# The experts' SiLU in a Mamba block with experts: one ScalarE function in place of tanh and a VectorE operation

## What is computed

```python
g = jnp.einsum('th,eih->tei', x, gate_proj)
u = jnp.einsum('th,eih->tei', x, up_proj)
act = jax.nn.silu(g) * u
expert_out = jnp.einsum('tei,ehi->teh', act, down_proj)
y = jnp.einsum('teh,te->th', expert_out, combine)
# and in the mixer, for each token:
A_bar = jnp.exp(dt_t[:, :, None] * A)
h = A_bar * h + (dt_t * x_t)[:, :, None] * B_t[:, None, :]
y_t = jnp.einsum('bdn,bn->bd', h, C_t)
```

## Time and profile before

| what | us |
|---|---|
| median of 3 runs (2777.73 to 2789.72) | 2781.56 |
| span of the profiled execution | 2779.7 |
| VectorE busy | 2424.8 |
| TensorE busy | 2379.4 |
| GpSimd busy | 2234.5 |
| ScalarE busy | 1565.3 |

### The profile page before, as it was taken

The page is one execution under the profiler, slowest core; times in us unless marked ns, Lnnn a source line. Parts: engine busy times, 40 slices in busy tenths (PEclk is TensorE's granted clock), DMA queues, the critical chain, the costliest instruction groups (busy, mean ns, idle before and its releaser), DMA issues.

```text
span 2779.7 us, 29004 instructions
## 1 busy us (share of the span) xinstructions
PE 2379.4 (86%) x9004; PEld 1687.3 (61%) x9004; DVE 2424.8 (87%) x2450; ACT 1565.3 (56%) x2961; POOL 2234.5 (80%) x1563
## 2 busy tenths in 40 slices
PE   3445798998989899898989999898999989898899
PEld 1222466666756666675666667666666756666678
DVE  2688999999999999999999999999999999999922
ACT  3556666566566656655665655566565556665311
POOL 1578888888888888888898888888888888987922
PEclk8677899999999899999999999999999999999999
DMA  4689898999989899998989989898998989898921
GB/s 113 172 209 231 220 236 219 229 237 218 239 221 235 218 227 235 222 236 214 234 224 238 232 220 244 213 233 218 241 231 218 241 205 235 222 245 210 241 64 50
DMA packets 338380, 596.80 MB, mean 215 GB/s; under 512 B 49696, under 2 KB 160288, under 8 KB 338224
## 3 DMA queue, kind: packets, MB, share of 16 engines
q0 software_dynamic: 72960, 243.30, 45.6%
q1 hardware_dynamic: 265264, 351.64, 40.3%
HBM read 349.89 MB, written 10.06 MB: 129 GB/s over the span
## 4 chain that ended last, share of the span: by engine, by line
PE 25%; POOL 22%; issue 17%; DVE 17%; ACT 10%; DMA 8%; SPq 0%; POOLq 0%; DVEq 0%; ACTq 0%
POOL unit L1199 9%; PE wbank L498 7%; DVE hbank L726 7%; DMA gsum<-unit 4%; POOL act L1166 4%; POOL gsum L1211 3%; PE mbank L510 3%; PE wbank L440 3%; DVE unit L740 3%; PE wbank L526 2%; PE wbank L388 2%; ACT z L849 2%; PE wbank L460 2%; DMA w_all<-w_scratch 2%; ACT hbank L1028 2%
## 5 line engine op out<-in xcount | busy, mean ns | idle before, releaser
L1199 POOL TENSOR_TENSOR unit<-dtx,b_bc 128x1024 f32<-128x1024 f32 x512 | 1345.9, 2639 | 10.8 <-DMA b_bc<-bc_scratch 8.9
L726 DVE TENSOR_TENSOR_SCAN hbank<-hbank,unit 128x1024 f32<-128x1024 f32 x512 | 1173.2, 2291 | 72.7 <-ACT hbank L1028 66.4
L1028 ACT ACTIVATE hbank<-dt,a_neg 128x512 f32<-128x512 f32 x1024 | 668.8, 681 | 303.6 <-DVE unit L740 269.6
L510 PE MATMUL mbank<-down_t,act 128*128 128x256 f32 x2048 | 525.6, 394 | 69.5 <-POOL act L1166 46.7
L740 DVE TENSOR_TENSOR unit<-hbank,c_bc 128x1024 f32<-128x1024 f32 x448 | 546.2, 1219 | 25.9 <-DVE hbank L726 1.8
L1166 POOL TENSOR_TENSOR act<-act,w_all 128x512 f32<-128x512 f32 x256 | 359.6, 1405 | 242.6 <-DVE act L704 222.9
L1211 POOL DMA_DIRECT2D gsum<-unit x448 | 444.0, 991 | 105.0 <-DMA gsum<-unit 50.8
L498 PE MATMUL wbank<-h_t,up_t 128*128 128x256 f32 x2048 | 503.6, 390 | 10.7 <-DVE gz L608 10.7
L510 PEld LDWEIGHTS mbank<-down_t,act 128*128 128x128 f32 x2048 | 397.5, 197 | 176.2 <-issue 64.8
L498 PE MATMUL wbank<-h_t,gate_t 128*128 128x256 f32 x2048 | 489.4, 382 | 13.4 <-DVE dt L600 11.4
L498 PEld LDWEIGHTS wbank<-h_t,up_t 128*128 128x128 f32 x2048 | 396.0, 195 | 108.8 <-DVE gz L608 29.2
(11 more groups left out here) (121 smaller groups left out, 2398.2 us busy)
## 6 DMA issues: line engine op xcount, KB each, us to landing
gsum<-unit POOLq DMA_DIRECT2D x448, 512.0 KB, 7.3
c_bc<-bc_scratch SPq DMA_DIRECT2D x464, 256.0 KB, 5.6
b_bc<-bc_scratch SPq DMA_DIRECT2D x448, 256.0 KB, 6.2
w_all<-w_scratch SPq DMA_DIRECT2D x256, 256.0 KB, 4.6
ht<-in_L_attn_x_dram SPq DMA_DIRECT2D x16, 512.0 KB, 6.0
w_out<-in_L_attn_W_out_dram SPq DMA_DIRECT2D x16, 512.0 KB, 6.2
ht<-in_L_attn_x_dram POOLq DMA_DIRECT2D x16, 512.0 KB, 8.4
out_dram<-xt SPq DMA_DIRECT2D x16, 512.0 KB, 3.3
```

Of the source, the lines that this page charges most:

```text
L510: m = eng.matmul(mbank[:, u * H:(u + 1) * H], act[:, (n - 1) % MOE_RING, j, u * P:(u + 1) * P], down_t[:, e, :], start=(e == 0 and u == 0) ...
L726: eng.tensor_tensor_scan(h, h, unit[:, g % RING, :, :].rearrange("p a t -> p (a t)"), 0.0, ALU.mult, ALU.add).then_inc(scanned, 1)
L1028: eng.activation(hbank[g % HB][:, a, :], dt[:, 2 * q + a, :], ACT.Exp, scale=a_neg[:, 2 * q + a, n:n + 1]).then_inc(decayed, 1)
L1199: eng.tensor_tensor(unit[:, g % RING, :, :], dtx[:, 2 * q:2 * q + 2, :], b_bc[:, s:s + 1, :].to_broadcast([P, 2, T]), ALU.mult).then_inc(d ...
```

## The change

The experts' function on ScalarE is Silu in place of tanh of half the value. It writes straight into `act` and frees the gate bank; the tile `etanh`, its semaphore and VectorE's (tanh + 1) * gate are gone. VectorE's product with the up product waits for Silu through the semaphore of the gate bank. The down weights are no longer halved. ScalarE has to load a table where it goes from Silu to Exp, Tanh or Ln and back.

```diff
--- before.py
+++ after.py
@@ -164,7 +164,6 @@
         rows_out = sb("rows_out", [BC, T])
         mod_row = conv[:, 1, :].rearrange("p (a h) -> p a h", h=H)
         act = sb("act", [P, MOE_RING, 2, HT])
-        etanh = sb("etanh", [P, 2 * HT])
         w_all = sb("w_all", [P, W_RING, 2, HT])
 
         sums = sb("sums", [P, TT])
@@ -231,8 +230,8 @@
         rnorm_a, rnorm_p, rnormed = sem("rnorm_a"), sem("rnorm_p"), sem("rnormed")
         driven, decayed, scanned, c_scaled = (sem(n) for n in ("driven", "decayed", "scanned", "c_scaled"))
         summed = [sem(f"summed{k}") for k in range(2)]
-        etanhed, weighted, down_done, moe_v, moe_out = (
-            sem(n) for n in ("etanhed", "weighted", "down_done", "moe_v", "moe_out"))
+        weighted, down_done, moe_v, moe_out = (
+            sem(n) for n in ("weighted", "down_done", "moe_v", "moe_out"))
         work = Banks(wbank, [sem(f"work{k}_full") for k in range(3)], [sem(f"work{k}_free") for k in range(3)])
 
 
@@ -690,15 +689,9 @@
                 for s in range(E + 1):
                     n = E * row + s
                     a = act[:, n % MOE_RING, :, :].rearrange("p j t -> p (j t)")
+                    yield
                     if s < E:
-
-                        t = work.at["gates2", row, s]
-                        need.wait_ge(etanhed, n + 1)
-                        eng.scalar_tensor_tensor(out=a, in0=etanh[:, :], scalar=1.0, in1=t.bank[:, :], op0=ALU.add,
-                                                 op1=ALU.mult).then_inc(t.free, 1)
-                    yield
-                    if s < E:
-                        g, t = t, work.at["ups2", row, s]
+                        g, t = work.at["gates2", row, s], work.at["ups2", row, s]
                         need.wait_ge(t.full, t.after)
                         need.wait_ge(g.free, g.after)
                         eng.tensor_tensor(a, a, t.bank[:, :], ALU.mult).then_inc(t.free, 1)
@@ -755,7 +748,7 @@
                     o = dst[:, 2:4, :].rearrange("p e h -> p (e h)") if split else dst[:, 2:4, :, :].rearrange(
                         "p e k i -> p (e k i)")
                     need.wait_ge(t.full, t.after)
-                    eng.tensor_scalar(o, t.bank[:, :], 0.5 if split else 1.0, None, ALU.mult).then_inc(t.free, 1)
+                    eng.tensor_copy(o, t.bank[:, :]).then_inc(t.free, 1)
                     yield
 
 
@@ -1012,10 +1005,8 @@
                     if s < E:
                         t = work.at["gates2", row, s]
                         need.wait_ge(t.full, t.after)
-                        if E * row + s:
-                            used = work.at["gates2", *divmod(E * row + s - 1, E)]
-                            need.wait_ge(used.free, used.after)
-                        eng.activation(etanh[:, :], t.bank[:, :], ACT.Tanh, scale=0.5).then_inc(etanhed, 1)
+                        eng.activation(act[:, (E * row + s) % MOE_RING, :, :].rearrange("p j t -> p (j t)"),
+                                       t.bank[:, :], ACT.Silu).then_inc(t.free, 1)
                     for _ in range(4):
                         yield
 
@@ -1034,7 +1025,7 @@
                     o = dst[:, 0:2, :].rearrange("p e h -> p (e h)") if split else dst[:, 0:2, :, :].rearrange(
                         "p e k i -> p (e k i)")
                     need.wait_ge(t.full, t.after)
-                    eng.activation(o, t.bank[:, :], ACT.Copy, scale=0.5 if split else 1.0).then_inc(t.free, 1)
+                    eng.activation(o, t.bank[:, :], ACT.Copy).then_inc(t.free, 1)
                     yield
                     yield
```

## The result

The changed kernel takes 2920.82 us (median of 4 runs, 2919.21 to 2922.52), the kernel before beside it 2782.5: ratio 1.0499, 95% interval 1.0481 to 1.0517. That is 138 us slower, where 58 was forecast: the direction held and the time lies in the range, but the size is 2.4 times the forecast one. Its profiled execution has a span of 2917.7 us. A median counts every execution, a ratio only those that agree; the two differ once, with Silu at place 11 alone, where one of four executions took 10132.89 us (it is also the profiled one, so nothing is read from that trace).

A forecast was written before the change was run, and what follows sets the result against it. VectorE, 93.8% busy, was taken to set the pace. Late places of 8.8 us per image less 4.8 of relief, times 14.6 images, gave 58 us; 2779.7 + 58 + 1.9 = 2840 us, range 2735 to 2960.

The forecast's parts named there:

- place 11: Second pair of step sizes: two loads, no idle time; VectorE's addition to dt comes 1.8 us per image late.
- the rival of a second time per switch: Each table switch holds ScalarE for a second time as long as the load, by emptying it: 3090 us; chance 0.02.
- The walk: Through one image, 1302 to 1462 us, asking how late each scan's decay becomes: 8.8 us per image in sum.
- places 5 to 7: First pair of step sizes: five added loads, partly hidden in idle time, make a scan 3.2 us per image late.
- place 15: Ahead of the second norm: a function and two decays make L849 and the routing 2.4 us per image late.
- place 1: First norm: the decays end 2.8 us later, their scan comes 1.4 us per image late.
- the relief: VectorE's dropped operation and waits: full 11.8 us per image, of which eight operations at 0.60, 4.8 us, counted as usable.
- VectorE sets the pace: Steady part: VectorE, busy 375.34 of 400 us (93.8%), bounds the kernel, with three others within 10% of it.
- ScalarE becomes the bound: ScalarE's 140 us of work plus 31 idle make an image 12 us longer: 180 us more, 2960 us; chance 0.18.
- Relief wins: VectorE's savings partly cover the late places: 2.6 us per image less, 38 us, so 2742 us; chance 0.18.
- the 85: Sign that ScalarE is the bound: its share of an image reaches 85% or more and VectorE's falls under 85%.

The follow-up runs named there:

- Silu at place 11 alone: Changed kernel with Silu only at place 11 of an image's 16 experts' places, Tanh straight to the activations elsewhere: 2808.65 us, ratio 1.0104.
- the six together: Changed kernel with Silu only at the six tight places (1, 5, 6, 7, 11, 15), Tanh straight to the activations elsewhere: 2900.78 us, ratio 1.0431.
- The ten other places: Changed kernel with Silu only at the ten loose places (0, 2, 3, 4, 8, 9, 10, 12, 13, 14), Tanh elsewhere: 2768.51 us, ratio 0.9957.
- the loads present: Kernel before with Silu in place of Tanh in its own buffer, VectorE's operation kept: 2934.48 us, ratio 1.0552; the changed kernel is 15 us faster.
- the run with six operations kept: Kernel before with Tanh straight to the activations at ten places, tanh and VectorE's operation kept at places 1, 5, 6, 7, 11, 15: 2781.34 us, ratio 1.0006.
- the run without switches: Changed kernel with Tanh in Silu's place, written straight to the activations, so no added table loads: 2767.17 us, ratio 0.9938.

## Why the prediction was right and wrong

**Right: what the loads are.** 456 more were counted from the order of work; the trace has 455 (269 + 235 + 64, 15 ahead of L912 and one at the start are 584, against 129). They last 1283 ns, with 0.01 to 0.02 us to either neighbour where ScalarE has nothing to wait for, so the rival of a second time per switch is out. By the drain of the Trainium skill (ScalarE: Activation LUTs, "What ACT_TABLE_LOAD costs") ScalarE would have had an estimated 1213 us more; it has 602. The prediction's "Silu takes as long as tanh" holds (597 ns against 588).

**Right: few late places carry the cost.** The walk's own numbers against the runs, in us per image: places 5 to 7, 3.2 against 3.8; place 11, 1.8 against 3.2; place 15, 2.4 against 3.1; place 1, 1.4 against 0.2 alone. In sum 8.8 against 10.3, and 137 / 14.6 = 9.4 with the six together, 156 / 14.6 = 10.7 with all. The ten other places, for which the walk had nothing, cost 0.3. That the sum is this close is in part luck: place 1 was too high and places 11 and 15 too low. At place 15 the trace has 2.3 at the scan whose decays stand behind the Silu, and 0.6 between scans 11 and 12, which the walk put all at the norm; whether that 0.6 is the norm or the clock (at 0.50 for 9.0 us there, 6.9 without the Silu) isn't shown.

**Wrong by half at place 11.** The walk took the 1.8 by which VectorE's addition to dt moves and let VectorE work off the rest with five operations less. There is nothing to work off: the six steps behind take 26.55 us in the kernel before and 26.58 in the changed one, and the whole 2.7 of ScalarE's longer chain stayed.

**Wrong: the relief, the term that was mis-sized.** The prediction took eight operations at 0.60, 4.8 us per image, as usable. The runs show 1.2 (17 us), 15 us with the loads present. It is also in the other place: the walk gave up the three operations at the first step sizes and the five behind the second, and counted on the other eight, seven of them at loose places; the run with six operations kept shows nothing for the ten loose ones by themselves. With the measured terms the sum is 10.7 - 1.2 = 9.5 per image, times 14.6 is 139 us: the measured 138. With 8.8 and 4.8 it was 58. Of the 80 us that are missing, (4.8 - 1.2) * 14.6 = 53 are the relief, (10.7 - 8.8) * 14.6 = 28 the late places.

The step behind this was "VectorE sets the pace": a busy share of 93.8% was read as if a saving on it were a saving of time. VectorE's waits for decays went from 66 to 148 us once its operation was gone. The stretches show it place by place. At places 8 to 10 the saving is real (21.6 to 20.2 us), but 0.8 of it is lost at place 11, where ScalarE's chain, which starts when TensorE's product comes, sets the distance of the scans; at 12 to 14 it is nothing, where TensorE is full; at 6 and 7 the stretch even grows by 0.4; at 15 and at 0 to 5 it is 0.7 together. Of the six tight places the operation at 11 can be read: it is worth some 0.9 us per image (17.8 against 16.9). For the other five it isn't shown which of them count, nor is it shown for each stretch what holds it.

The clock of TensorE was in no term of the prediction. It went from 0.94 over the whole execution to 0.915. That isn't what most of the 138 us are: between scans 29 and 31 of an image in the changed kernel it is low for 5.6 us and in the run without switches for 0.7, and the scans stand at the same distances (4.87 and 4.13 us). Between scans 11 and 12, where the changed kernel has 0.7 us more, it can have a part.

**The rivals.** "ScalarE becomes the bound" is not it: with the ten loose places it was 76% busy in the steady stretch at no cost, and in the changed kernel it has 81% there, under the 85 that was named as the sign. "Relief wins" was to decide below 4.8 us of late places per image; with the measured relief it would have needed less than 1.2. That the time lies in the range says little for the forecast, as the range's upper end was taken from the first of these.

## What to carry to other kernels

Cost a table switch by where it stands, not by how many there are: 293 added loads cost 5 us at ten places, and 163 cost 137 us at six others, the clearest of which has ScalarE running through without a gap. Walk one period of the in-order engine and ask for each step by how much its product may come late; that found the costly places. Don't book a saving on the busiest engine as time when others are within 10% of it: ask what is late next at every place where it falls, or take the operation out alone and measure.

## What the runs showed of the hardware

- Silu and Tanh share a table: where the gates' tanh (L938 in the changed kernel) stands behind a Silu, at 15 of 64 places, it has no load of its own, and the load comes at the next decay. So the description of the change is wrong to have a load from Silu to Tanh. Exp and Tanh share one too (the kernel before has loads around Ln alone), so Tanh is in both.
- Taking work off one engine gave a fraction of it each time: 168 us of ScalarE gave 17, 200 us of GpSimd 31, 140 us of VectorE 17, and 128 us of TensorE 9, with the granted clock down from 0.94 to 0.91.
- A load of a table takes 1283 ns and is only as dear as its place: it raised ScalarE's busy time by 1.32 us each (602 us for 455), and the kernel's time by 5 us for 293 of them and by 137 us for 163.
